# Row fetches of the expert layers paced by points of the slots, and GpSimd issuing four of the first operand rows of the attention

## The reference

```python
x = L0_attn_x                                             # (4, 512, 128)
x = x + 0.5 * ffn(layernorm(x), Wg, W1, b1, W2, b2)       # E = 8 experts, F = 512, top 1
x = x + attn(layernorm(x), w_qkv, w_ky, w_proj)           # 16 heads of 8 channels
x = x + 0.5 * ffn(layernorm(x), Wg, W1, b1, W2, b2)

def ffn(x):
    prob = softmax(x @ Wg.T); e = argmax(prob)            # one expert for each token
    return (gelu(x @ W1[e].T + b1[e]) @ W2[e].T + b2[e]) * prob[e]

def attn(x):
    L, L_y = q @ k.T * scale, q @ k_y.T * scale
    agg = sum(exp(clip(L_y, -15, 15)) * mask) + EPS
    w = softplus(log(abs(L) + EPS) - log(agg + EPS)) * mask
    return (w / (sum(w) + EPS)) @ v @ w_proj.T
```

## Time and profile before

| | |
|---|---|
| median of 3 runs | 431.45 us (429.27 to 434.72) |
| the profiled execution | 431.77 us |
| its span, first to last instruction | 428.8 us |
| busy: PE, DVE, ACT, POOL | 327.0, 311.8, 297.5, 143.5 us |

### The profile page before, as it was taken

One profiled execution on the slowest core, in us unless ns is written; L12 is line 12 of the kernel. 1 busy time (PEld: TensorE's weight loads), 2 busy tenths in 40 slices (PEclk: granted clock), 3 DMA queues, 4 the chain that ended last, 5 costly groups with the idle time before them and its releaser, 6 DMA issues.

```text
span 428.8 us, 8272 instructions
## 1 busy us (share of the span) xinstructions
PE 327.0 (76%) x2376; PEld 199.1 (46%) x2376; DVE 311.8 (73%) x667; ACT 297.5 (69%) x862; POOL 143.5 (33%) x230
## 2 busy tenths in 40 slices
PE   6878999546876546778688587876888888789992
PEld 6638999523243211222224233232343574489992
DVE  5762444377879999999998999998999367334431
ACT  2814556414989999999999879997787653255551
POOL 7174545400334470025020240202530014744452
PEclk9988999858589755887967889799999956989998
DMA  8684656133477997003000030000300474546540
GB/s 243 216 260 126 208 168 170 49 98 131 138 201 205 228 236 140 0 2 99 2 0 2 0 98 2 2 0 2 98 2 2 124 264 106 161 145 188 161 138 24
DMA packets 37992, 47.60 MB, mean 111 GB/s; under 512 B 4288, under 2 KB 26816, under 8 KB 37696
## 3 DMA queue, kind: packets, MB, share of 16 engines
q1 hardware_dynamic: 33616, 36.20, 31.1%
q0 software_dynamic: 2560, 6.30, 4.9%
q10 hardware_dynamic: 1776, 4.60, 3.1%
HBM read 24.02 MB, written 6.29 MB: 71 GB/s over the span
## 4 chain that ended last, share of the span: by engine, by line
PE 33%; ACT 24%; DVE 20%; issue 12%; DMA 4%; SPq 2%; POOL 1%; another core or an unknown queue 1%; DVEq 0%; POOLq 0%; ACTq 0%
ACT R L873 10%; PE PS L1413 8%; PE PS L1423 7%; ACT R L881 5%; DVE R L1214 5%; ACT CL L873 5%; PE PS L1556 3%; DVE R L1199 3%; PE PS L1348 2%; DVE CL L1199 2%; ACT R L768 2%; PE PS L1538 2%; PE PS L1339 2%; PE PS L1569 1%; DMA R<-rows_d,R 1%
## 5 line engine op out<-in xcount | busy, mean ns | idle before, releaser
L1214 DVE TENSOR_TENSOR R<-PS,MB 128x1024 int32<-128x1024 int32 (+1 forms) x96 | 98.1, 1039 | 6.7 <-PE PS L1538 6.5
L768 ACT ACTIVATE R<-PS,R 128x128 f32<-128x128 f32 x184 | 52.8, 370 | 55.2 <-PE PS L1413 32.6
L881 ACT ACTIVATE R<-R 128x1024 f32<-128x1024 f32 x64 | 80.2, 1262 | 9.3 <-DVE R L1214 9.3
L873 ACT ACTIVATE R<-R 128x384 f32<-128x384 f32 (+2 forms) x192 | 77.4, 409 | 5.2 <-DVE R L1199 5.2
L1523 PE MATMUL PS<-R 64*128 64x512 bf16 (+3 forms) x256 | 40.7, 372 | 33.3 <-DVE CL L1199 15.3
L1199 DVE SCALAR_TENSOR_TENSOR R<-PS,MA 128x1024 f32<-128x1024 f32 x64 | 59.9, 952 | 1.0 <-PE PS L1523 0.8
L1556 PE MATMUL PS<-R,V 128*32 128x256 f32 (+3 forms) x512 | 54.0, 507 | 8.0 <-ACT R L881 8.0
L1413 PE MATMUL PS<-R 128*128 (+1 forms) x368 | 53.3, 289 | 7.2 <-DVE R L1084 6.5
L1413 PEld LDWEIGHTS PS<-R 128*128 128x128 f32 x368 | 46.2, 197 | 9.9 <-issue 7.2
L1423 PE MATMUL PS<-R 128*128 (+1 forms) x368 | 49.7, 279 | 0.7 <-ACT R L768 0.7
L1538 PE MATMUL PS<-QPS,R 64*128 64x512 bf16 (+3 forms) x256 | 37.4, 341 | 13.3 <-DVE R L1199 9.8
(11 more groups left out here) (168 smaller groups left out, 472.3 us busy)
## 6 DMA issues: line engine op xcount, KB each, us to landing
R<-w SPq DMA_DIRECT2D x38, 258.0 KB
R<-R SPq DMA_DIRECT2D x32, 128.0 KB, 2.4
R<-R SPq DMA_DIRECT2D x16, 256.0 KB, 6.4
QPS<-R SPq DMA_DIRECT2D x32, 128.0 KB, 2.5
R<-w ACTq DMA_DIRECT2D x8, 258.0 KB
rows_d<-X SPq DMA_DIRECT2D x8, 256.0 KB, 4.1
R<-w ACTq DMA_DIRECT2D x1, 2048.0 KB, 8.3
rows_d<-R SPq DMA_DIRECT2D x8, 256.0 KB, 2.3
```

The source lines that it names most:

```text
L768: last = act.activation(HT[:, k % 2, c * P:(c + 1) * P], PS[:, k % 2, c * P:(c + 1) * P], ACT.Gelu, bias=W1[:, k, F + c:F + c + 1])
L873: act.activation(e, e, ACT.Exp, scale=SCALE, accum_out=aggf[:, ds(s + (2 * i + par) * STEPS, 1)])\
L881: act.activation(w, w, ACT.Ln, bias=1.0, scale=1.0).then_inc(s_ln, 1)
L1214: dve.tensor_tensor(weights(v)[:, :, at:at + n].bitcast(i32), PS[:, SLOTS[slot(b_fill(v, g))], 0:n].bitcast(i32), spread(mask, 1, 2), ALU. ...
```

## The change

1. `gather`: 4 transfers instead of 6 wait for nothing. Tiles 4, 5 and 6 wait for `up` of slots 0, 1 and 2. From tile 7 on, four tiles go with three slots, each tied to another point: tiles 7, 11, 15 to `slot_out` of slots 1, 4, 7; tiles 8, 12 to `down` of slots 2, 5; tiles 9, 13 to the transpose of tiles 5, 8; tiles 10, 14 to `up` of slots 5, 8.
2. `scatter_back`: tiles 0 to 12 wait for `down` of slot t+8 too.
3. Of the 16 first half rows, GpSimd issues four on a semaphore of its own (`s_stkp`): key term 0 (3 rows), as soon as the term is ready, and the second key row of term 2. ScalarE is left with key term 1 (3 rows), SyncE with the 8 query rows and one key row of term 2. TensorE and `first_term` of ScalarE wait for the new semaphore too.

```diff
@@ -28,8 +28,9 @@
 W1_W = F + FC
 RING = 4
 
-
-AHEAD = 6
+FETCHED, FASTER = 4, 7
+
+LATER = 12
 NS = NT + E - 1
 H, HD = 16, 8
 HP = H // 2
@@ -67,6 +68,9 @@
 J_OFF = {0: 0, 3: 512, 1: 640, 2: 1024}
 HEAD_W = 1280
 STACK_DMAS = 16 * PRODUCTS
+
+POOL_ROWS = 4
+FIRST_STACK_DMAS = STACK_DMAS, STACK_DMAS - 16 * POOL_ROWS
 
 A_AT = HP - 1
 R_AT = A_AT + 1
@@ -320,6 +324,7 @@
         s_stk = [sem(f"stack_{i}_written") for i in range(len(STACKS))]
 
         s_stk0 = [sem(f"stack_{i}_first_half_written") for i in range(2)]
+        s_stkp = sem("stack_1_first_half_rows_by_gpsimd")
         s_wh = sem("half_wise_weights_ready")
         s_qv = sem("qv_done")
         s_qc = sem("q_copied")
@@ -456,20 +461,20 @@
                         sp.dma_start(QPS[stack_rows(t), (b + 1) % 2, :, :], QP3[:, term, :])\
                             .then_inc(s_qps, 16)
 
-            def half_stack(i, half, terms=(0, 1, 2)):
+            def half_stack(i, half, terms=(0, 1, 2), some=slice(0, 3)):
 
                 dst = (QS, YS)[i]
                 written = (s_stk0, s_stk)[half][i]
                 for term in terms:
                     sp.wait_ge((s_hi, s_mid, s_lo)[term], i + 1)
-                    for t in rows_of(K_TERMS if i else Q_TERMS, term):
+                    for t in rows_of(K_TERMS if i else Q_TERMS, term)[some]:
                         sp.dma_start(dst[stack_rows(t), half * HP // 2:(half + 1) * HP // 2, 0:SEQ],
                                      SP3[0][half * P // 2:(half + 1) * P // 2, term, i * SEQ:(i + 1) * SEQ])\
                             .then_inc(written, 16)
 
             half_stack(0, 0)
 
-            half_stack(1, 0, (2,))
+            half_stack(1, 0, (2,), slice(0, 1))
             for i in range(2):
                 half_stack(i, 1)
             for i in range(2, 7):
@@ -559,13 +564,32 @@
                 pool.tensor_tensor(ex, sh, spread(lnt[:, 2, :].rearrange("p (n o) -> p n o", o=1), 2, E),
                                    ALU.mult).then_inc(s_shr, 1)
 
+            def fetch_in_slot(r, t):
+
+
+                n, k = divmod(t - FASTER, 4)
+                if t < FASTER:
+
+                    pool.wait_ge(s_up, r * NS + t - FETCHED + 1)
+                elif k == 0:
+
+                    pool.wait_ge(s_y, r * NS + 3 * n + 2)
+                elif k == 1:
+
+                    pool.wait_ge(s_dn, r * NS + 3 * n + 3)
+                elif k == 2:
+
+                    pool.wait_ge(s_px, r * NT + 3 * n + 6)
+                else:
+
+                    pool.wait_ge(s_up, r * NS + 3 * n + 6)
+
             def gather(r):
                 pool.wait_ge(s_src, r + 1)
                 pool.wait_ge(s_xnd, 2 * 16 * NB * (r + 1))
                 for t in range(NT):
-                    if t >= AHEAD:
-
-                        pool.wait_ge(s_px, r * NT + t - AHEAD + 1)
+                    if t >= FETCHED:
+                        fetch_in_slot(r, t)
                     pool.indirect_dma_start(XS[:, t, :], None, rows_d,
                                             bass.IndirectOffsetOnAxis(source[:, t:t + 1], 0))\
                         .then_inc(s_xl[t], 16)
@@ -574,6 +598,9 @@
                 for t in range(NT):
 
                     pool.wait_ge(s_y, r * NS + t + E)
+                    if t <= LATER:
+
+                        pool.wait_ge(s_dn, r * NS + t + E + 1)
                     to = bass.IndirectOffsetOnAxis(source[:, t:t + 1], 0)
                     if r == 0:
                         pool.indirect_dma_start(x_d, to, XS[:, t, P:2 * P], None).then_inc(s_xd, 16)
@@ -601,6 +628,16 @@
             def third_term(m):
                 pool.wait_ge(s_mid, m + 1)
                 pool.tensor_tensor(term_of(m, 2), REM[:, m % 2, :], term_of(m, 1), ALU.subtract).then_inc(s_lo, 1)
+
+            def first_keys(term, rows):
+
+                pool.wait_ge((s_hi, s_mid, s_lo)[term], 2)
+                for t in rows:
+                    pool.dma_start(YS[stack_rows(t), 0:HP // 2, 0:SEQ], SP3[0][0:P // 2, term, SEQ:2 * SEQ])\
+                        .then_inc(s_stkp, 16)
+
+            first_keys(0, rows_of(K_TERMS, 0))
+            first_keys(2, rows_of(K_TERMS, 2)[1:])
 
             done = [0]
 
@@ -804,8 +841,9 @@
                 if u == 4:
 
                     for i in range(2):
-                        act.wait_ge(s_stk0[i], STACK_DMAS)
+                        act.wait_ge(s_stk0[i], FIRST_STACK_DMAS[i])
                         act.wait_ge(s_stk[i], STACK_DMAS)
+                    act.wait_ge(s_stkp, 16 * POOL_ROWS)
                 if u == 5:
 
                     for i in (2, 3):
@@ -840,7 +878,6 @@
             first_term(1)
             for m in range(2):
                 second_term(m)
-            first_keys(0, s_hi)
             first_keys(1, s_mid)
             copy_xnt(1, 1, 3, XNT2)
             tables(EXP_AND_LN)
@@ -1630,7 +1667,8 @@
                 v = s - LAG
                 if s == 0:
                     for i in range(2):
-                        pe.wait_ge(s_stk0[i], STACK_DMAS)
+                        pe.wait_ge(s_stk0[i], FIRST_STACK_DMAS[i])
+                    pe.wait_ge(s_stkp, 16 * POOL_ROWS)
                 if s == HP // 2:
                     for i in range(2):
                         pe.wait_ge(s_stk[i], STACK_DMAS)
```

## The result

| | before | after |
|---|---|---|
| median of 13 runs each | 432.12 us (429.27 to 434.72) | 429.71 us (428.23 to 431.22) |
| ratio, with 95% interval | | 0.9939 (0.992 to 0.9958) |
| the profiled execution | 431.77 us | 430.58 us |
| its span | 428.8 us | 428.7 us |

The changed kernel is 2.4 us faster, 0.6%, clear of chance by its interval. The prediction was 430.9 us in a range from 426.9 to 433.8, with 0.5 us gained; the time is inside the range. Most of the steps behind it were wrong nevertheless: the gain came from a place where the sum held nothing, and in three places the change costs time.

What follows compares the result with a forecast made beforehand. TensorE was taken to bound the slots, and SyncE's ten row issues and one landing the attention's start. Parts 1 and 2 counted 0, part 3 a gain of 0.5: 431.45 - 0.5 = 430.9 us, range 426.9 to 433.8.

Steps and rivals of the forecast that it cites:

- The bound in the slots: Expert-layer slots: TensorE is full, 4.00 of 4.00 us; row fetches count only if late or disturbing TensorE or VectorE.
- Part 1, cost 0: Expert-layer fetches: pacing them neither costs nor gains; the tightest, tile 6, has 3.3 us to spare.
- late-fetch rival: Expert layers: a paced fetch comes late, 0.6 us in each layer, giving 432.2 us; chance 0.08.
- the rival said 3.9: Second layer's start: unpaced fetches disturb TensorE there, pacing gives back 3.9 us, for 427.0 us; chance 0.18.
- its own falsifier: Expert-layer slots: the prediction is wrong if they change by more than 0.05 us each, 2 us over both layers.
- Part 2, cost 0, at most 0.02: Last scatters of each layer: the later waits are covered by 0.4 us in the first, used up in the second.
- the start of tile 12: End of each layer: the last delayed scatter starts at 78.7 and 418.6, after `down` of slot 20.
- if a step were 0.2 longer: Last scatters: with GpSimd's steps that much above 1.25 us, the second layer would end 0.6 us later.
- Part 3, 0.5 us: Start of the attention: sharing out the row issues starts the scores at 103.75 instead of 104.25, gain between 0.05 and 0.65.
- lands at 101.41 + 2.07: Start of the attention: SyncE's last row, issued 0.63 us earlier, lands at 103.48 with its old landing time.
- The port rival: Start of the attention: GpSimd's descriptors and VectorE block each other, scores 1.5 us later, 433.0 us; chance 0.12.
- The sum: Whole program: only part 3's 0.5 us counts, 431.77 to 431.3 for the profiled execution, 430.9 us for the median.

Runs made afterwards that it cites:

- e6: The kernel before run against itself, nothing changed, in a slow group; ratio 0.9985.
- e9: The kernel before with part 2 alone, the later scatters, in a slow group; ratio 0.9996 against the kernel before.
- e5: The changed kernel again, all three parts, measured in another slow group; ratio 0.9896 against the kernel before.
- e12: The changed kernel with the waits of tiles 9, 10, 13 and 14 moved to part fetch pairs; ratio 0.9906 against the kernel before, in a slow group.
- slow groups: Groups of runs, the main comparison among them, in which the kernel before takes 432.1 to 432.8 us and its second layer has the gap.
- quick group: The first group of follow-up runs, in which the kernel before takes 423.2 us and no profile shows the gap.
- e1: The kernel before with part 1 alone, the paced fetches, in the quick group; ratio 1.0034 against the kernel before.
- e11: The kernel before with all sixteen fetches waiting for nothing (`AHEAD = 16`); ratio 1.0515 against the kernel before, 22.8 us slower.
- e2: The kernel before with part 2 alone, the later scatters, in the quick group; ratio 1.0061 against the kernel before.
- e3: The kernel before with part 3 alone, four first rows issued by GpSimd, in the quick group; ratio 1.0041 against the kernel before.

## Why the prediction was right in its number and wrong in its steps

**The bound in the slots, "they count only if they disturb TensorE".** The condition was put, and then answered from the wrong place. The window of 45 to 49 us, TensorE 4.00 of 4.00 busy, is a paced stretch already, where tile t waits for the transpose of tile t-6. The unpaced series is at the start of the layer, and there the rows showed a hole of 3.93 us.

**Part 1, cost 0.** Right that no transpose waits for a late fetch: the late-fetch rival did not occur. Wrong that there was nothing to gain. Between the first and the third `up` of the second layer the change brought 2.87 us, where the rival said 3.9, and 1.5 more in the two slots behind it, where the clock had fallen. Against that rival I had set that the first layer's chain has no such hole. It had a smaller one, hidden in the products of the coefficients. The chain of waits, first layer, before and after:

```profile
34.76 2.16 PE PS L1392 x16
...
35.00 0.93 PE PS L1429 x16
```

The reader of these products started 1.28 us after their modelled end before, 1.07 in `e6` and 1.00 in `e9`, and 0.04 after. I looked for an entry without a releaser instead. The 0.80 us of the first layer's start in the table above are not the measure of it. The granted clock was 0.50 from 32.1 to 35.5 before and from 30.2 to 37.1 after, and of two kernels with the same pace of the first fetches `e5`, at 1.00 throughout, took 3.99 us there and `e12`, at 0.50 from 31.5 to 38.3, 6.33. The rival was right about the place and the cause, and had a chance of 0.18.

**The slots.** The text named its own falsifier, slots changing by more than 0.05 us each, 2 us over both layers. Over both layers the profile went from 103.3 to 100.8 us, 2.5 us or 0.054 a slot. It is no even change: two stretches at the starts shorter by 0.80 (in part the clock's) and 2.87, and short stops in the middle, of which the first layer's make +1.85. The unpaced fetches of before had their stops at the start, the paced ones have some in the middle.

**Part 2, cost 0, at most 0.02.** Mis-sized, 0.58 us at the end of the second layer. The step that failed is the start of tile 12: I let it start at 418.6, 0.2 us after the `slot_out` at 418.41 began. After, it starts 418.06 - 417.39 = 0.67 us after that `slot_out`'s start, and the steps are 1.27, not 1.25. With both, the old profile's numbers give 418.41 + 0.67 + 3 x 1.27 = 422.89 for the last scatter, against 422.33: 0.56 late, as measured. The delay of the start is a matter of the second wait: tile 12's wait for `down` (L603) was over at 417.3, and its issue started at 418.06, where a scatter with one wait starts 0.28 us after its release. The 0.67 is the same in all six kernels with the new scatters. The text had said what it would cost "if a step were 0.2 longer"; that is the same 0.6 by another route. What it missed altogether is that part 2 belongs to part 1: it parts the two series of GpSimd.

**Part 3, 0.5 us.** Mis-sized: between 0.2 gained and 0.2 lost, and it costs 0.34 elsewhere. By its own steps: SyncE's last issue 0.63 earlier was 0.48; GpSimd's issues, bounded by 0.63 and 1.25 us each, took 1.64 / 3 = 0.55, under the lower bound, so the indirect form was the wrong row to take; ScalarE's copy ended 104.18 - 96.62 = 7.56 after the query term, near the 7.7 forecast. The step that failed is "lands at 101.41 + 2.07": the landing was carried over from a time in which two queues fed the DMA engines. With GpSimd's beside them it took 2.67, and 0.6 is what the step had gained. In the four profiles with the rows this landing took 2.45 to 2.67. From query term to scores it takes 8.94 to 9.12 us in the ten profiles without the rows, 9.02 and 9.00 of them in the kernel before, and 8.81, 8.86, 9.25 and 9.03 in those with the rows.

**The port rival** (433.0) did not occur. The twelve L1017 took 3.16 us, the same as before. But the change put it to less of a test than the rival had in mind: GpSimd's issues were short, and only the fourth, from 101.40 to 101.98, fell among the twelve, of which each took 0.34 us; the first three ran beside other work of VectorE, where the two L1213 took 1.47 us. The rule of the Trainium skill, "SBUF — State Buffer", section "Who interferes with whom", by which GpSimd's descriptors and VectorE in a two-port mode hold each other up, does not show at this place; that VectorE was in such a mode here, no run shows.

**The late fetch** (432.2) was also added up wrongly: 0.6 in each layer and 0.6 at the end less 0.5 on 431.45 is 432.75. And by the diff the lead grows to seven slots at tile 15, not eight. Neither changes the forecast.

**The sum.** For the profiled executions: 0.24 - 0.80 + 1.85 + 0.11 + 0.23 + 1.08 - 0.24 - 2.87 - 0.65 + 0.93 = -0.12, the difference of the spans. That the medians differ by 2.4 us and these two executions only by 1.2 in time is the spread of single executions; the attention's +1.08 has no step of the change in it, and that stretch ran from 233.3 to 237.0 us in the profiles of the slow groups. The +1.85 in the first layer is of the change: the other kernels with paced fetches have 45.2 to 46.3 us there in the slow groups, against 43.7 before. (In the quick group `e1` has 43.6.) That 430.9 came close to 429.7 is luck: gains and losses that the sum didn't hold nearly cancel.

**Left open.** How GpSimd's issuing stops TensorE, what sets it free, and why in some groups of runs and not in another: the chip, its state at the time and where the buffers lay are all untested. That it comes from the fetches' descriptors rather than from their packets is suggested by the low DMA share in `e11`, but nothing was run that tells them apart. The four scatters issued back to back at 418.06 (and at 80.46 in the first layer) stop nothing, which a complete account would have to explain. In the quick group parts 1, 2 and 3 alone lose 0.3, 0.6 and 0.4% (1.4 to 2.6 us), of which 0, 0.6 and 0.3 us are found; all three parts together were not measured there, so whether the change is a gain under such conditions isn't known.

## What to carry to other kernels

When an engine is full in the middle of a stage, look at the distances of its first few steps too: a series of transfers issued ahead of a stage can disturb its start and not its middle, and a chain entry without a releaser is a finding to be priced, not noise. When such distances are compared, the granted clock of the stretch has to be compared with them: here it fell behind a stop and stretched the next two slots. Before a queue is relieved by sharing its issues out, ask what the landings will be once all of them are in flight together, and never carry a landing time over from a quieter moment. A delay that ends in a program's last transfers is paid in full, so the last items of a series shouldn't inherit the waits of the others.

## What the runs showed of the hardware

- With GpSimd issuing sixteen indirect transfers of 128 rows without a break (`e11`), TensorE's finished work was not signalled for 10.7 us in one layer, and for 5.5 and 4.3 in the other. In another group of runs thirteen in a row had no effect (`e2`, `e3`).
- After such a stop the granted clock fell to 0.50 for 3.4 to 6.8 us (before, `e6`, `e9`): 19 matmuls in 3.40 us instead of 31.
- The long stops have no releaser in the profile: the entry is "another core or an unknown queue" in the chain and "remote" in the timeline. The short ones are put down to the matmul itself, as the 1.57 us at 45.75. Both are seen by a reader that waits long after the modelled end of the matmul.
- A plain transfer of 64 rows of 1 KB within SBUF costs GpSimd 0.55 us to issue, about what it costs SyncE (0.54 to 0.73 in the same stretch); an indirect one of 128 rows 0.95 and 1.25 from start to start.
- With GpSimd's queue beside those of SyncE and ScalarE the busy share of the DMA engines rose from 0.60 to 0.94 at the same 205 GB/s, and the landing of a row from 2.07 to 2.67 us.
- Where a scatter had two waits instead of one, 0.7 us passed between the end of the second and the issue, instead of 0.28.
- Four plain transfers from GpSimd early in the program lengthen its closing wait, 300 us later, by 0.34 us, in every profile that has them.
